# Replacing the up-front copy of x into the output by indirect scatters of only the rows that no expert serves

## What is computed

```python
h = einsum(x, W[cat_ids]) + b[cat_ids]         # one 512x512 matrix for each of the 4 sequences
probs = softmax(h @ Wr); eidx = argmax(probs)  # 8 experts, one for each token
rank = position of the token among the tokens of its expert
keep = rank < cap                              # cap = 4096 / 8 = 512 slots for each expert
ye = relu(h[dispatch] @ W1[e]) @ W2[e]         # 512 -> 2048 -> 512, for each expert
out = x + scatter(ye * prob * valid)
```

## Time and profile before

| | |
|---|---|
| median of three runs | 873.74 us |
| the profiled execution, its own time | 873.38 us |
| its span in the trace | 871.7 us |
| TensorE busy | 850.4 us, 98% of the span |
| VectorE, ScalarE, POOL busy | 49%, 30%, 24% |
| DMA | 126.86 MB, 146 GB/s in the mean |

### The profile page before, as it was taken

One profiled execution on the slowest core, in us unless ns is written; L12 is line 12 of the kernel. 1 busy time (PEld: TensorE's weight loads), 2 busy tenths in 40 slices (PEclk: granted clock), 3 DMA queues, 4 the chain that ended last, 5 costly groups with the idle time before them and its releaser, 6 DMA issues.

```text
span 871.7 us, 10460 instructions
## 1 busy us (share of the span) xinstructions
PE 850.4 (98%) x3952; PEld 690.1 (79%) x3953; DVE 426.7 (49%) x640; ACT 257.4 (30%) x361; POOL 205.8 (24%) x205
## 2 busy tenths in 40 slices
PE   8999999799999999999999999999999999999994
PEld 5777777588888888888888888888888888888883
DVE  4586677236343634363436343634363436343632
ACT  3322211223222322232223222322232223222320
POOL 1000000730730073007300731073007300030001
PEclk9898999999999999999999999999999999999997
DMA  8784755732444244424342444244424432242001
GB/s 295 294 316 163 281 204 234 232 128 97 140 151 147 97 140 151 144 98 143 141 145 97 139 150 144 98 137 151 147 97 138 157 135 96 99 152 94 0 0 48
DMA packets 54201, 126.86 MB, mean 146 GB/s; under 512 B 5752, under 2 KB 5752, under 8 KB 53538
## 3 DMA queue, kind: packets, MB, share of 16 engines
q1 hardware_dynamic: 42674, 93.35, 31.1%
q0 software_dynamic: 10928, 32.16, 10.4%
q10 hardware_dynamic: 576, 1.05, 0.4%
HBM read 110.13 MB, written 25.17 MB: 155 GB/s over the span
## 4 chain that ended last, share of the span: by engine, by line
PE 94%; DMA 2%; SPq 1%; DVE 1%; issue 1%; POOL 0%; ACT 0%; POOLq 0%; DVEq 0%
PE acc_ps L843 40%; PE y_ps L826 40%; PE acc_ps L759 7%; PE tp_ps L759 3%; PE tp_ps L705 2%; PE y_ps L690 2%; DMA b_col<-cond_b 1%; DMA rows<-h_rows,tok_all 1%; PE y_ps L738 0%; POOL out L360 0%; SPq L244 0%; PE y_ps L714 0%; DVE rows L507 0%; DVE rows L674 0%; SPq L213 0%
## 5 line engine op out<-in xcount | busy, mean ns | idle before, releaser
L843 PE MATMUL acc_ps<-xt_split,w_split 128*128 128x512 f32 x1536 | 367.8, 389 | 1.1 <-DVE xt_split L627 1.1
L826 PE MATMUL y_ps<-w_split,xt_split 128*128 128x512 f32 x1536 | 367.6, 389 | 0.0
L843 PEld LDWEIGHTS acc_ps<-xt_split,w_split 128*128 128x128 f32 x1536 | 288.2, 188 | 61.1 <-DVE xt_split L627 1.2
L826 PEld LDWEIGHTS y_ps<-w_split,xt_split 128*128 128x128 f32 x1536 | 288.3, 188 | 59.8
L651 DVE SCALAR_TENSOR_TENSOR xt_split<-acc_ps,xt_split 128x512 fp32r<-128x512 f32 x128 | 88.6, 692 | 314.7 <-ACT xt_split L456 314.7
L456 ACT ACTIVATE xt_split<-acc_ps 128x512 fp32r<-128x512 f32 x128 | 76.5, 598 | 401.6 <-PE acc_ps L843 401.6
L335 POOL DMA_INDIRECT rows<-h_rows,idx_all x112 | 122.8, 1097 | 265.5 <-DVE tp_ps L641 233.0
L568 DVE TENSOR_TENSOR w_split<-stage,w_split 128x1024 fp32r<-128x1024 f32 x66 | 80.9, 1226 | 19.3 <-ACT w_split L407 19.3
L574 DVE TENSOR_TENSOR w_split<-stage,w_split 128x1024 fp32r<-128x1024 f32 x66 | 80.9, 1226 | 16.4 <-ACT w_split L413 16.4
L360 POOL DMA_INDIRECT out<-rows,put_all x32 | 32.0, 999 | 222.8 <-DVE rows L674 217.6
L759 PE MATMUL acc_ps<-w_split,xt_split 128*128 128x512 f32 x264 | 70.8, 422 | 1.0 <-DVE w_split L487 1.0
(11 more groups left out here) (85 smaller groups left out, 258.2 us busy)
## 6 DMA issues: line engine op xcount, KB each, us to landing
stage<-w SPq DMA_DIRECT2D x64, 1024.0 KB, 5.3
stage<-x_t SPq DMA_DIRECT2D x7, 1024.0 KB, 8.0
h_rows<-rows POOLq DMA_DIRECT2D x7, 1024.0 KB, 8.2
stage<-cond_wt SPq DMA_DIRECT2D x4, 1024.0 KB, 7.8
stage<-cond_w SPq DMA_DIRECT2D x3, 1024.0 KB, 6.4
rows<-h_rows,idx_all POOLq DMA_INDIRECT x112
stage<-x_t ACTq DMA_DIRECT2D x4, 256.0 KB, 3.4
stage<-cond_w SPq DMA_DIRECT2D x4, 256.0 KB, 3.0
```

Source lines behind the costliest of these rows:

```text
L826: last = nc.tensor.matmul(y_ps[:, s, :], hts[:, j % 2, a, s * P:(s + 1) * P], w2s[:, slot, w, kk, :], start=(j == 0 and (a, w) == (HI, HI) ...
L843: last = nc.tensor.matmul(acc_ps[:, j % 2, :], w1s[:, slot, w, k, jj * P:(jj + 1) * P], xts[:, par, a, k, :], start=(k == 0 and (w, a) == ...
```

## The change

The four copies and POOL's wait for them go. SP loads, once for each expert number e, the e-th 512 rows of x (1 MB, in order of tokens, not by expert) into `b_rows`, the former buffer of bias rows. POOL scatters them in four parts of 128 rows; tokens with a slot get an index that is 8192 too high, and their rows are left out. The indices need the ranks of all tokens, so `rank` becomes `place_all` for all 32 tiles, and `make_tables` has four more instructions. One buffer is used for all loads: SP waits for the scatters of e-1 before it loads part e, at the head of the weight loads of expert e.

```diff
-        rank = sb("rank", [P, TPC], f32)
+        place_all = sb("place_all", [P, NT], f32)
+        drop_f = sb("drop_f", [P, NT], f32)
+        drop_all = sb("drop_all", [P, NT], u32)
...
-        s_keep = sem("x_copied")
+        s_xrow = sem("x_rows_loaded")
+        s_drop = sem("dropped_rows_written")
...
+        x_v = x.rearrange("(e t p) d -> p e t d", p=P, t=BATCH)
...
-            def copy_x(b):
-
-                n = TOKENS // BATCH
-                sp.dma_start(out[b * n:(b + 1) * n, :], x[b * n:(b + 1) * n, :]).then_inc(s_keep, 16)
...
-                copy_x(b)
...
-            copy_x(0)
...
+            def load_x_rows(e):
+                sp.dma_start(b_rows[:, :, :], x_v[:, bass.ds(e, 1), :, :].rearrange("p o t d -> p (o t) d")
+                             ).then_inc(s_xrow, 16)
...
             with sp.Fori(0, E - 1) as e:
+                sp.wait_ge(s_drop, e * (16 * BATCH))
+                load_x_rows(e)
                 for q in range(QN):
                     load_later(e, q)
+            sp.wait_ge(s_drop, (E - 1) * (16 * BATCH))
+            load_x_rows(E - 1)
             for q in range(QN - 2):
                 load_later(E - 1, q)
...
-            pool.wait_ge(s_keep, 16 * BATCH)
             for e in range(E):
...
                 if e + 2 < E:
                     pool.wait_ge(s_tp, DK * (e + 2))
                     gather_quarters(e + 2)
+                pool.wait_ge(s_xrow, 16 * (e + 1))
+                for t in range(BATCH):
+                    pool.indirect_dma_start(
+                        out=out, out_offset=bass.IndirectOffsetOnAxis(ap=drop_all[:, BATCH * e + t:BATCH * e + t + 1],
+                                                                      axis=0),
+                        in_=b_rows[:, t, :], in_offset=None,
+                        bounds_check=TOKENS - 1, oob_is_err=False).then_inc(s_drop, 16)
...
                 pool.wait_ge(s_put, 16 * SB * (e + 1))
+                pool.wait_ge(s_drop, 16 * BATCH * (e + 1))
...
-                then(nc.vector.tensor_reduce(rank[:, :], ranks[:, :, :], AX.X, ALU.add))
+                then(nc.vector.tensor_reduce(place_all[:, tiles], ranks[:, :, :], AX.X, ALU.add))
...
                 then(nc.vector.tensor_copy(tok_all[:, :, :], tok_f[:, :, :]))
+                then(nc.vector.scalar_tensor_tensor(drop_f[:, :], payload[:, :, 0], float(P), payload[:, :, 1],
+                                                    ALU.mult, ALU.add))
+                then(nc.vector.tensor_scalar(place_all[:, :], place_all[:, :], float(CAP), float(SKIP),
+                                             ALU.is_lt, ALU.mult))
+                then(nc.vector.tensor_tensor(drop_f[:, :], drop_f[:, :], place_all[:, :], ALU.add))
+                then(nc.vector.tensor_copy(drop_all[:, :], drop_f[:, :]))
```

More of the change, by code:

```diff
@@ L557, in place @@
                                              onehot[:, par, :, :], ALU.mult))
-                then(nc.vector.tensor_reduce(rank[:, :], ranks[:, :, :], AX.X, ALU.add))
+                then(nc.vector.tensor_reduce(place_all[:, tiles], ranks[:, :, :], AX.X, ALU.add))
                 for t in range(TPC):
-                    last = nc.vector.tensor_scalar(select[:, par, t, :], iota_c[:, :], rank[:, t:t + 1], None,
+                    last = nc.vector.tensor_scalar(select[:, par, t, :], iota_c[:, :], place_all[:, TPC * c + t:TPC * c + t + 1], None,
                                                    ALU.is_equal)
```

## The result

Twenty runs of each kernel gave a median of 876.10 us for the changed one (873.06 to 878.98) against 873.84 us for the one before (870.93 to 876.73). The ratio is 1.003, with a 95% interval of 1.002 to 1.004: 2.3 us slower, under the 0.5% that the prediction called telling, but clear of the interval. The profiled execution of the changed kernel took 877.38 us with a span of 875.7 us, 4.0 us more than the one of before.

What follows compares the result with a forecast made beforehand. TensorE was taken as the bound, busy for 98% of the span. All terms were 0 except +0.31 us for the four table instructions, added to the median of 873.74 us: 874.0 us, range 869.6 to 877.3 us.

Steps and rivals of the forecast that it cites:

- Bound and copies: Whole kernel: TensorE bounds it, busy 98% of the span; removing the four hidden copies gains 0, bounds -1.5 to 0 us.
- the second rival: After the first copy: copies slow three groups of twelve matmuls; removing them saves 7 us, giving 867 us; chance 0.05.
- Tables: Routing stage, VectorE: four new instructions take 0.92 us, 0.61 of it in idle time: +0.31 us, bounds 0 to +0.92.
- SP's loads and its wait: Expert loop: x loads and later weight loads cost 0; in expert 2 they land by 345.4 us, needed at 359.38.
- the upper bound: Expert 2: with scatters of 2.08 us each and longest landings, loads land by 357.5 us, still before 359.38.
- The first rival: Experts 1 to 6: slow scatters delay weight loads, 3 us lost in each, 18 in all: 892 us; chance 0.07.
- POOL's 32 scatters: Each expert: four scatters take 5.2 us on POOL, hidden in its 10.96 us of idle time: cost 0.
- Tail: End of kernel, from the last result scatters: the last part of x was scattered about 70 us before, so cost 0.
- the sum's own bounds: Whole kernel: the forecast time before allowing for variation of medians, from 872.2 to 874.7 us.
- the start of the first expert: After the gather: first expert matmul at about 163.0 us if right, more than 1 us away if wrong.

Runs made afterwards that it cites:

- the second run with 223 DMAs: The kernel before with 36 empty scatters in a row in expert 7, run once more: 875.42 us, ratio 1.0025.
- the disturbed chip: Chip of four runs adding 16 or 36 empty scatters to the kernel before, 8 scatters or 8 plain copies to the changed one; kernel before took 882.47 us there.

## Why the prediction was right, and where not

*Bound and copies: right.* TensorE's stretch of an expert stayed at 87.0 us and its routing stage at 154.0 us busy. Up to 150 us it waits for no load after the first groups, and without the copies nothing got faster: the ratio without copies, loads and scatters is 0.9998. One size was wrong without effect on the sum: the copies are 8.39 MB of the 126.86 MB that the page counts (118.47 MB without them), not 16.8. And the groups of twelve matmuls that take 5 us, on which the second rival rested, are a matter of the clock: in the kernel before, the two of the earlier trace rows ran at a granted clock of 0.50 and 0.54, a group of 2.89 us at 30.22 us at 1.00 (windows as in the earlier trace rows, the granted clock third from the end):

```profile
22.72:28.21 5.49, 5.49 (x16) 4.08 (x14) 0.43 (x3) 0.00 (x0) 0.00 (x0) 0.50 0.76 278
30.22:33.10 2.88, 2.88 (x14) 2.12 (x12) 0.00 (x0) 2.24 (x4) 0.38 (x1) 1.00 1.00 403
68.42:73.63 5.21, 5.21 (x19) 3.97 (x19) 1.89 (x11) 2.83 (x6) 0.00 (x0) 0.54 0.00 0
```

These 0.50 and 0.54 stand for the lower level, for all or nearly all of the window. In the changed kernel, without any copy, they still take 5.49 and 4.92 us.

*Tables: right in kind, smaller in size.* The term of 0.31 us measured 0.05. The idle time of 0.61 us was used up as forecast; the rest is accounted for by an overlap of about 0.1 us between instructions that follow each other on VectorE without a gap. The last entry of the tables starts at 146.94 and lasts 0.21, yet `store_h` starts at 147.06, and the next two steps follow in the same way.

*SP's loads and its wait: right.* Forecast release 334 us, measured 332.93; no split waits for weights. The 32 scatters took 0.98 to 1.19 us each; the lengthening to 2.08 us that the upper bound allowed for did not show. The first rival, weights late, did not come.

*POOL's 32 scatters: hidden where forecast, but the step that failed stands right behind.* "Tail. It begins with the last result scatters. The last part of x was scattered about 70 us before: 0." The tail is not only what is issued in it. POOL's closing drain depends on the DMAs that POOL has issued in the whole kernel, and 32 more made it 3.59 us longer. The term put at 0 was the largest of all. The forecast, +0.3 us against a measured +2.3, held the time only thanks to its range, whose upper end, 877.3, owes 2.6 us to the variation of medians (the sum's own bounds ended at 874.7); neither rival had this mechanism. In that the forecast was lucky.

*What stays open.* The drain is 3.6 us longer in all three traces with 219 DMAs, while the medians differ by 2.3 and, the second time, by 2.6. Some 1.0 to 1.3 us comes back elsewhere. The kernel with copies and tables, 0.9982 with an interval up to 0.9998, is a candidate for a gain that I can't name. Against this size stand variations between executions of any kernel: the second condition tile starts between 11.9 and 14.3 us, the first expert matmul between 159.3 and 164.6, and the 2.6 us at the lower clock come in some executions at the start of expert 0. Twelve to twenty runs of each do not part these. For the same reason the start of the first expert, within 1 us of 163.0 us here (163.2), was no sign of the forecast being right.

## What to carry to other kernels

A DMA that POOL issues can have a price at the end of the kernel, even where its issue and its transfer are hidden (here 0.0817 us for each one added in expert 7, and 3.59 us for the 32 of the change, as long as the drain had not fallen back): ask the trace for the closing block's lines before costing a tail at nothing, and compare that drain first when a change in the number of POOL's DMAs moves a kernel by a few us. Where the copy is hidden, as here, replacing it by something finer on POOL gains nothing: the 8.4 MB of copies cost nothing that the runs show. The doubled scatters, 0.5% under the kernel before, are a finding and not a design: 2.0 of the 4.3 us come from where the queue happens to stand at the end, the rest is not explained, and the better lever, fewer DMAs on POOL, was not tried here.

## What the runs showed that was not expected

- POOL's closing drain takes 0.0817 us for each DMA added (5.631, 6.937 and 8.571 us with 187, 203 and 223), is the same to the nanosecond in kernels that issue the same number in the same order (9.224 in three traces, 5.631 in three, 8.571 in two), doesn't depend on a DMA's packets (3.344 and 3.339 us with scatters of 80 packets or copies of 8 bytes), and falls back between 223 and 227 DMAs (8.571 us with 223; 2.936 to 3.344 with 227, 3.671 with 251). That the queue has filled up there is inferred.
- POOL stands still for 2.54 us with no wait in two of the kernels whose drain fell back, both at their 224th DMA. With a burst of eight in expert 7 the same 227 DMAs ended with 3.34 us and no standstill in the tail.
- A scatter of 128 rows that are all left out takes POOL 1.0 us, as a full one does, and lands in 2.1 us in the median (36 of them in the second run with 223 DMAs), against 2.8 us for the result scatters of before.
- TensorE had a low-clock stretch at the start of expert 0 in some executions, after the gather, at a cost of 2.6 us (experts' stage 698.8 instead of 696.2 us): in the traces of the two kernels with copies and tables, and in all four of the disturbed chip, where the stage took 699.6 to 743.7 us and the clock fell only some 10 us into the expert in two; in none of the others. Its cause was not looked for.
